# Rows of x turned on VectorE, from quarter rows, in a gated attention and mixture-of-experts kernel

## The reference

```python
router_logits = flat @ router_w.T                 # flat: 4096 rows (xn), 16 experts
topk_w, topk_idx = jax.lax.top_k(softmax(router_logits), 2)
topk_w = topk_w / jnp.sum(topk_w, axis=-1, keepdims=True)
shared = silu(flat @ shared_gate_w) * (flat @ shared_up_w) @ shared_down_w   # inner width 1024
# each expert, on the rows that chose it, inner width 512:
dn = (silu(xs @ gate_w[e]) * (xs @ up_w[e])) @ down_w[e]
routed = zeros.at[sorted_tok].add(sorted_w[:, None] * dn)
output = shared + routed                          # then gated by g_ffn and added to the row
```

## Time and profile before

| | |
|---|---|
| median of 3 runs | 3086.06 us (3083.86 to 3086.15) |
| the profiled execution | 3110.33 us, span 3108.8 us |
| TensorE matmul, busy | 2960.7 us (95%) |
| VectorE, busy | 1638.6 us (53%) |
| ScalarE, busy | 1013.8 us (33%) |
| GpSimd, busy | 595.8 us (19%) |
| mean granted TensorE clock | 0.979 |

### The profile page before, as it was taken

How to read it: one execution, slowest core, us unless ns; L and a number is a source line. 1 busy time by engine, 2 the same in 40 slices (tenths; PEclk the granted TensorE clock), 3 DMA queues, 4 the chain that set the end, 5 groups by cost and what they waited for, 6 DMA issues and landing times.

```text
span 3108.8 us, 48018 instructions
## 1 busy us (share of the span) xinstructions
PE 2960.7 (95%) x17262; PEld 2443.7 (79%) x17263; DVE 1638.6 (53%) x3104; ACT 1013.8 (33%) x1916; POOL 595.8 (19%) x572
## 2 busy tenths in 40 slices
PE   4799999999999988999999999999999999999999
PEld 3687777777878766888888888888888888888887
DVE  3778788887888764333243333332333344444444
ACT  4444444444444412332233333332333331111111
POOL 1333333333343331000000000000000001111111
PEclk6799999999999998999999999999999999999999
DMA  6454445445444534143433333433333324444444
GB/s 192 137 170 137 150 137 176 151 140 158 152 150 142 153 128 152 59 149 128 142 141 136 142 135 142 142 135 142 140 143 135 135 81 158 145 138 159 142 145 145
DMA packets 205721, 441.74 MB, mean 142 GB/s; under 512 B 86784, under 2 KB 87680, under 8 KB 205056
## 3 DMA queue, kind: packets, MB, share of 16 engines
q1 hardware_dynamic: 110544, 333.62, 31.7%
q0 software_dynamic: 24400, 72.96, 7.2%
q10 hardware_dynamic: 70656, 33.56, 4.2%
HBM read 350.72 MB, written 107.18 MB: 147 GB/s over the span
## 4 chain that ended last, share of the span: by engine, by line
PE 59%; DVE 1%; ACT 1%; ACTq 0%; issue 0%; DVEq 0%
PE p_g_b L1532 19%; PE p_up_b L1532 19%; PE p_y_b L1520 17%; PE p_x_b L1500 3%; PE p_h_b L1507 1%; DVE w_lo L1384 1%; ACT w_hi L1327 1%; ACTq L1181 0%; ACTq L1166 0%; DVE x L1440 0%; DVE sg_b L1412 0%; DVE x L1431 0%; ACT th_b L1369 0%; DVE y_b L1442 0%; ACTq L1323 0%
## 5 line engine op out<-in xcount | busy, mean ns | idle before, releaser
L1400 DVE TENSOR_TENSOR ht_lo_b<-p_h_b,ht_hi_b 128x512 fp32r<-128x512 f32 x105 | 72.4, 689 | 544.5 <-ACT ht_hi_b L1339 544.5
L1532 PE MATMUL p_g_b<-w_hi,xt_hi_b 128*128 128x512 f32 x840 | 342.0, 407 | 16.2 <-DVE w_lo L1384 12.9
L1520 PE MATMUL p_y_b<-w_hi,ht_hi_b 128*128 128x512 f32 x840 | 340.1, 405 | 1.9 <-DVE ht_lo_b L1400 1.9
L1412 DVE SCALAR_TENSOR_TENSOR sg_b<-th_b,p_g_b 128x512 f32<-128x512 f32 x105 | 72.1, 687 | 493.5 <-ACT th_b L1369 493.5
L1532 PE MATMUL p_up_b<-w_hi,xt_lo_b 128*128 128x512 f32 x840 | 331.0, 394 | 0.0
L1532 PE MATMUL p_up_b<-w_lo,xt_hi_b 128*128 128x512 f32 x840 | 330.1, 393 | 0.0
L1520 PE MATMUL p_y_b<-w_lo,ht_hi_b 128*128 128x512 f32 x840 | 330.0, 393 | 0.0
L1532 PE MATMUL p_g_b<-w_hi,xt_lo_b 128*128 128x512 f32 x840 | 329.8, 393 | 0.0
L1532 PE MATMUL p_up_b<-w_hi,xt_hi_b 128*128 128x512 f32 x840 | 327.4, 390 | 0.0
L1532 PE MATMUL p_g_b<-w_lo,xt_hi_b 128*128 128x512 f32 x840 | 327.0, 389 | 0.0
L1520 PE MATMUL p_y_b<-w_hi,ht_lo_b 128*128 128x512 f32 x840 | 326.8, 389 | 0.0
(11 more groups left out here) (221 smaller groups left out, 5694.1 us busy)
## 6 DMA issues: line engine op xcount, KB each, us to landing
mid_y<-y_b SPq DMA_DIRECT2D x73, 512.0 KB, 3.2
stage<-mid_g_row SPq DMA_DIRECT2D x64, 512.0 KB, 5.4
stage<-in_eg SPq DMA_DIRECT2D x16, 2048.0 KB
stage<-in_eu SPq DMA_DIRECT2D x16, 2048.0 KB, 15.2
stage<-in_ed SPq DMA_DIRECT2D x16, 2048.0 KB, 19.4
mid_y<-in_x SPq DMA_DIRECT2D x34, 512.0 KB
stage<-in_x SPq DMA_DIRECT2D x32, 512.0 KB
stage<-in_ctx_t ACTq DMA_DIRECT2D x32, 512.0 KB, 8.3
```

Of the source, the lines that this page charges most:

```text
L1400: nc.vector.tensor_tensor(ht_lo[:, :, :], p_h[:, :, :], ht_hi[:, :, :].bitcast(f32), ALU.subtract).then_inc(ht_rdy, 1)
L1412: nc.vector.scalar_tensor_tensor(out=sg[:, :], in0=th[:, :], scalar=1.0, in1=p_g[:, :], op0=ALU.add, op1=ALU.mult).then_inc(silu_step, 1)
L1520: last = nc.tensor.matmul(p_y[n][:, :], a[:, k, :], b[:, GUP + k, w], start=(k == 0 and m == 0), stop=(k == FE // P - 1 and m == 2))
L1532: mm = nc.tensor.matmul(out[:, :], a[:, k, :], w[:, k, o:o + FE], start=(k == 0 and m == 0), stop=(k == KD - 1 and m == 2))
```

## The change

The rows of x are no longer turned on TensorE but on VectorE, in blocks of 32 by 32, each of which stays in its group of 32 partitions. So the parts of a row are spread over the four groups when they are loaded: group a (partitions 32a to 32a + 31) gets quarter a of every row, four tokens to a partition. One instruction then turns all of it, into `x_t` in SBUF, where partition p holds the values 8p to 8p + 7. The weights' rows are loaded in the same order ("(p k) f" in place of "(k p) f"), since value 8p + k now meets slice k.

For this, `idx` is loaded four times, once for each group, and a number 0 to 3 (`quarter`) is added on GpSimd, which gives rows of xn seen as 16384 quarter rows (the lists now hold four times the token). Four gathers of 128 quarter rows of 1 KB follow in place of one of 128 rows of 4 KB. Plain loads of x are four as well, one for each group of 32 partitions. The turn stands in VectorE's body between `h_low` and `silu_up`. `x_high` and `x_low` read `x_t` in place of PSUM. `sg` is gone: silu works in `th`.

```diff
@@ mix_block, end of GpSimd's part
-            pool.dma_start(idx[:, :], t["lists"][0:P, :]).then_inc(idx_in, 16)
-            ge_apart(pool, past, (idx_in, 16), (xn_out, 16 * NCH), (xn_ps, 2 * NCH))
-            nc.gpsimd.indirect_dma_start(
-                out=xn[:, :], out_offset=None, in_=t["xn"],
-                in_offset=bass.IndirectOffsetOnAxis(ap=idx[:, :], axis=0)).then_inc(row0_in, 16)
+            for a in range(4):
+                pool.dma_start(idx[32 * a:32 * a + 32, :], t["lists"][0:P, :].rearrange("(j t) w -> j (t w)", t=4)
+                               ).then_inc(idx_in, 16)
+            ge_apart(pool, past, (quarter_set, 4))
+            pool.wait_ge(idx_in, 64)
+            nc.gpsimd.tensor_tensor(idx_q[:, :], idx[:, :], quarter[:, :], ALU.add).then_inc(idx_rdy, 1)
+            ge_apart(pool, past, (xn_out, 16 * NCH), (xn_ps, 2 * NCH))
+            pool.wait_ge(idx_rdy, 1)
+            for n in range(4):
+                nc.gpsimd.indirect_dma_start(
+                    out=xn[:, 256 * n:256 * n + 256], out_offset=None,
+                    in_=t["xn"].rearrange("c (a d) -> (c a) d", a=4),
+                    in_offset=bass.IndirectOffsetOnAxis(ap=idx_q[:, n:n + 1], axis=0)).then_inc(row0_in, 16)
@@ weights_in
-        eng.dma_start(place, matrix.rearrange("(k p) f -> p k f", p=P)).then_inc(sem, 16)
+        eng.dma_start(place, matrix.rearrange("(p k) f -> p k f" if place.shape[1] == GUP else "(k p) f -> p k f", p=P)
+                      ).then_inc(sem, 16)
@@ ffn_block, plain loads of x (SyncE's load_x, GpSimd's first two)
+            for a in range(4):
+                eng.dma_start(xg_parts[32 * a:32 * a + 32, :, :], xn_quarters[c, a]).then_inc(done, 16)
@@ ffn_block, GpSimd's rows_of
-                    ge_apart(pool, past, (x_in, 16 * i))
-                    pool.dma_start(idx[:, :], list_parts[bass.ds(part, 1)].rearrange("o p w -> (o p) w")
-                                   ).then_inc(idx_in, 16)
-
-                ge_apart(pool, past, (idx_in, 16 * i + 16 if c is None else 0), (xt_ps, i))
+                    for a in range(4):
+                        pool.dma_start(idx[32 * a:32 * a + 32, :],
+                                       list_parts[bass.ds(part, 1)].rearrange("o (j t) w -> (o j) (t w)", t=4)
+                                       ).then_inc(idx_in, 16)
+                    ge_apart(pool, past, (idx_in, 64 * i + 64))
+                    ge_apart(pool, past, (x_in, 64 * i))
+                    nc.gpsimd.tensor_tensor(idx_q[:, :], idx[:, :], quarter[:, :], ALU.add).then_inc(idx_rdy, 1)
+                    ge_apart(pool, past, (idx_rdy, i + 1))
+                ge_apart(pool, past, (x_turned, i))
@@ ffn_block, VectorE
+            def turn_x(i, c):
+
+                ge(dve, xt_rdy, 2 * i)
+                if c is None or isinstance(c, int) and c == 0:
+                    dve.wait_ge(x_in, 64 * i + 64)
+                else:
+                    dve.wait_ge(xs_in, 64 * c)
+                nc.vector.transpose(x_t[:, :, :].rearrange("p k (j t) -> p t k j", t=4),
+                                    xg_parts[:, :, :].rearrange("p t (i k) -> p t k i", k=KD)).then_inc(x_turned, 1)
...
                 if prev:
                     h_low(i)
+                if not last:
+                    turn_x(i + 1, c)
                 silu_up(i)
@@ ffn_block, TensorE
                 mm.then_inc(gu_ps, 1)
-                if not last:
-                    turn_x(i + 1, c)
                 if prev:
                     down(i, e - 1 if first else e)
```

More of the change, by code:

```diff
@@ L166, in mix_block @@
         cnt_ps, cnt_step = sem("cnt_ps"), sem("cnt_step")
-        idx, idx_in, row0_in = keep["idx"], keep["idx0_in"], keep["row0_in"]
+        idx, idx_q, quarter = keep["idx"], keep["idx_q"], keep["quarter"]
+        idx_in, idx_rdy, row0_in = keep["idx0_in"], keep["idx0_rdy"], keep["row0_in"]
         gu0_hi, gu0_split = keep["gu0_hi"], keep["gu0_split"]
         xn_out = sem("xn_out")
-        fill_in = sem("fill_in")
+        fill_in, quarter_set = sem("fill_in"), sem("quarter_set")
         wp_in = [sem(f"wp_in{n}") for n in range(SLOTS)]
@@ L660, in stage_w @@
                                             ).then_inc(w_split, 1)
+                if part == 1 and b == 0 and j == 2:
+                    for a in range(4):
+                        nc.vector.memset(quarter[32 * a:32 * a + 32, :], a).then_inc(quarter_set, 1)
             def stage_l(part, b, j):
@@ L1131, in ffn_block @@
         base_row = sb("base_row", [P, D])
-        p_x = [ctx.enter_context(nc.psum_tensor(f"p_x{n}_{tag}", [P, 4, P], f32)) for n in range(2)]
         p_g = ctx.enter_context(nc.psum_tensor(f"p_g_{tag}", [P, FE], f32))
@@ L1137, in ffn_block @@
         r0, r1 = keep["x1"][:, 0, :], keep["x1"][:, 1, :]
-        idx, starts_i = keep["idx"], keep["starts_i"]
+        idx, idx_q, quarter, starts_i = keep["idx"], keep["idx_q"], keep["quarter"], keep["starts_i"]
         first_row = sb("first_row", [P, NE])
@@ L1341, in x_high @@
             def x_high(i):
-                act.wait_ge(xt_ps, i + 1)
+                act.wait_ge(x_turned, i + 1)
                 for n in range(2):
-                    nc.scalar.activation(xt_hi[:, 4 * n:4 * n + 4, :], p_x[n][:, :, :], ACT.Copy).then_inc(xt_hi_rdy, 1)
+                    nc.scalar.activation(xt_hi[:, 4 * n:4 * n + 4, :], x_t[:, 4 * n:4 * n + 4, :],
+                                         ACT.Copy).then_inc(xt_hi_rdy, 1)
             def y_left(q):
@@ L1483, in finish @@
                 join(q, c)
+            turn_x(0, None)
             x_low(0)
@@ L1490, in _ @@
             trio = ((xt_hi, w_hi), (xt_lo, w_hi), (xt_hi, w_lo))
-            def turn_x(i, c):
-                if c is None or isinstance(c, int) and c == 0:
-                    pe.wait_ge(x_in, 16 * i + 16)
-                else:
-                    pe.wait_ge(xs_in, 16 * c)
-                for k in range(KD):
-                    last = nc.tensor.transpose(p_x[k // 4][:, k % 4, :], xg[:, k * P:(k + 1) * P], ident[:, :])
-                last.then_inc(xt_ps, 1)
             def turn_h(i):
@@ L1559, in build @@
         for n, s, dt in (("stage", [P, PIECES, D], f32), ("w_hi", [P, PIECES, D], f32r), ("w_lo", [P, PIECES, D], f32r),
-                         ("xn", [P, D], f32), ("x1", [P, 2, D], f32), ("idx", [P, 1], i32), ("starts_i", [P, 2, NE + 1], i32)):
+                         ("xn", [P, D], f32), ("x1", [P, 2, D], f32), ("idx", [P, 4], i32), ("quarter", [P, 4], i32), ("idx_q", [P, 4], i32), ("starts_i", [P, 2, NE + 1], i32)):
             keep[n] = ctx.enter_context(nc.sbuf_tensor(n, s, dt))
-        for n in ("idx0_in", "row0_in", "gu0_hi", "gu0_split"):
+        for n in ("idx0_in", "idx0_rdy", "row0_in", "gu0_hi", "gu0_split"):
             keep[n] = ctx.enter_context(nc.semaphore(n))
```

35 lines of the change are left out of this document (20 added, 15 removed).

## The result

The changed kernel took 2988.85 us in the median of four runs (2987.68 to 2991.48), the kernel before 3084.96 us on the same chip: ratio 0.9693, 95% interval 0.9682 to 0.9705. That is 96.1 us off, where 84.3 were forecast.

A forecast was written before the change was run, and what follows sets the result against it. TensorE's own work was taken to bound the kernel; -89.6 us for removed transposes and +4.6 at the start gave -85.0, scaled to 84.3 off 3086.06: 3001.7 us, 8-in-10 range 2991 to 3027.

The forecast's parts named there:

- the removal per tile: TensorE, routed stage: without eight transposes the down products move up 0.87 us in 103 tiles, 89.6 us in all.
- the overlap at the two ends: TensorE, either end of a tile's transposes: by how overlap is counted, the removal could be 0.79 to 0.95 us.
- The turn: VectorE, between ht_lo and silu: one turn of x a tile, taken as 2.0 us, bounds 1.2 to 5.5, costing nothing.
- The cover: VectorE's idle time before silu plus room behind it: a turn up to 7.0 us, 6.1 in a first tile, is free.
- Rival D: VectorE: strides make the turn slow, each us past 7.0 paid 103 times, about 3210 us at 9; chance 0.03.
- The gathers: GpSimd: four gathers a tile, 1.27 us apart, land 9.0, at worst 12.2 us after a turn, within 14.9; cost nothing.
- Rival C: GpSimd: each gather lasts its full landing time, so the period becomes 20.4 us and the time near 3245; chance 0.04.
- their ring: Routed tiles: a turn frees the next gathers, whose landing allows the next turn; decides from a period of 18.1 us on.
- Rival B: Tiles beside weight loads: x is late only there, 30 us if two tiles of 15 experts lose 1 us; chance 0.08.
- The start: Routed stage's opening: idx loads, gathers and turn are not hidden, first gate product +4.6 us, bounds +3 to +8.
- nothing given: Routed stage's second tile: transposes lie beside the tanh and silu chain in a pause that stays, so removing them gains nothing.
- The scaling to the median by 0.9922: Whole kernel: unprofiled median is 0.9922 of the profiled time, so -85.0 us became 84.3 off 3086.06.

The follow-up runs named there:

- the longer index buffers: Kernel before with idx as wide as in the changed kernel and quarter and idx_q allocated but unused: ratio 0.9958 to the kernel before.
- three turns: Changed kernel with every tile's turn of x done three times over on VectorE, 6.9 us in place of 2.27: 3064.06 us.
- the run with eight gathers: Changed kernel with four spare gathers, into a buffer that nothing reads, ahead of the four in each routed tile: 3017.76 us.
- the one with twelve: Changed kernel with eight spare gathers, into a buffer that nothing reads, ahead of the four in each routed tile: 3322.0 us.
- the other chip: Changed kernel itself, repeated on the chip of later experiments: ratio 0.969 to the kernel before.
- the changed kernel with the shorter start: Changed kernel with idx's four groups filled by one transfer and tile 1's list fetched ahead of the routed stage: 3001.58 us beside the changed kernel's 3003.78.
- the kernel before with 128 bytes: Kernel before with longer index buffers and 64 bytes more of unused memory, its operands moved by 128 bytes in all: ratio 1.0097 to the kernel before.
- 512 bytes added: Changed kernel with 512 bytes of unused memory ahead of x_t: ratio 0.9672 to the kernel before.
- 96 bytes: Changed kernel with 96 bytes of unused memory ahead of quarter: ratio 0.9861 to the kernel before.
- its repeat: Kernel before, unchanged, profiled again: ratio 0.9994.

## Why the prediction was right, and where its range failed

The way of the change and its mechanism were right, and the experiments bear them out; the step that failed is the size of the first term, the removal per tile.

**The removal.** The step "the down products move up by the whole 0.87 us" held, in 103 tiles. The term was mis-sized: tiles gave 0.99, not 0.87 (0.95 at most), so -101.6 us and not -89.6. Of the 0.12 missing, 0.08 is the place in memory, of which the forecast said nothing, and 0.00 to 0.04 the overlap at the two ends, for which its bound of 0.95 had room. That is, it took the longer index buffers for bytes without a price. The eight transposes cost 0.87 to 0.91 us by experiment, 0.11 each. The Trainium skill, "TensorE: Matmul & The Clock Gate", Part 4, gives about 275 ns for one of bf16 in a kernel; the record's length agrees (272 ns), the price of one in a row of eight does not, and 2.2 us a tile were not there to gain.

**The turn.** 2.27 us where 2.0 were taken, inside the bounds, wholly in the idle stretch. The cover was 7.4 us (forecast 7.0) in a plain tile, and less at an expert's change, where three turns already cost. Rival D would have needed 7.5 us or more. Taking the strides' 1.02 us away left the tile at 16.81 us, so the turn's length does not set the time. The Trainium skill, "Advanced Engine Details and Errata", SBUF Cachelines, has the penalty without a figure. The strided row that I held against it shows little of one: 345 ns less the fixed 154 is 1.5 ns an element for 1.2. The turn does show one: strides of 32 and 16 bytes took 1.0 ns an element on top of 1.2; which of the two strides costs it, no run tells.

**The gathers.** Issue at 1.27 us apart, x late in no plain tile, as forecast. Rival C fell: twice as many cost nothing in a plain tile, and only with twelve does their ring set the period throughout. Rival B's direction was right for eight and twelve gathers, not for four.

**The start.** Forecast +4.6, measured +4.0 to the first product. That it came so near is partly luck. The forecast let x's landing, 4.4 us behind the last gather's start, set the first turn; what set it was the end of the block, 7.2 us behind that start (0.95 of issue and 6.24). And it put the last gather 11.7 us behind the first idx load, where it was 8.6. The two errors nearly cancel. What failed is the silence on the tile after: the forecast costed the first tile's x and then counted tile 1 as "nothing given", where its chain (four idx loads, four gathers, of which one took 1.89 us beside w_lo, a landing of 6.48 us beside weight loads) is longer than tile 0's products. It cost 3.7 us more, 0.9 of it through the clock. On the other chip tile 1's period was 17.94 us, 1.9 more than 16.07, so the size varies. The last tile gave 1.7 back: the last 24 down products took 7.41 us before, in a stretch granted 0.77 of the clock, and 5.78 after, granted 1.00. The change did not do that: both values turn up in both kernels (7.33 us at 0.77 in the changed kernel with the shorter start, 5.87 us at 1.00 in the kernel before with 128 bytes), in all four behind a pause of 1.8 to 1.9 us.

**The ledger** in the profiled executions: stretch of 104 periods 1768.8 - 1866.7 = -97.9 (which is -101.6 and tile 1's +3.7), the first stage's last store to the first tanh +3.96 - 0.32 = +3.6, behind the last tanh 17.5 - 19.2 = -1.7. The sum is -96.0, and the medians differ by 96.1; so close a match is partly chance, since the -1.7 is the clock's and not the change's. From the forecast's -85.0 to it, the removal makes -12.0, tile 1 +3.7, the start -1.0 and the clock in the last tile -1.7. The scaling to the median by 0.9922 was needless: as far as the profiles tell, what the profiled execution of before had over its median lay in the first stage, since the routed stage took 1866.7 us in it and again when it was repeated. It moved the forecast by 0.7 us. The low end, 2991, rested on 0.95 us a tile with +3 at the start; 0.99 was outside it.

## What to carry to other kernels

Work taken from the engine that bounds comes back at its price in the chain, and what takes its place is free up to a room that can be read beforehand; but read the room in the tightest tile, not the plain one, walk the first tiles of a stage one by one, and count what is issued ahead of a block's end, since the engines wait for that. When buffers change size, ask what moves behind them: here 32 bytes decide over 1.5% of the time, half of what this whole change gave, so two kernels are compared at equal places, or a spread of places is tried with unused memory.

## What the runs showed of the hardware

A product of 512 columns starts every 227.6 to 228.9 or every 233.1 to 234.2 ns by the place of the routed buffers in memory. Ten kernels fit a rule by the remainder of the address by 512 bytes, and one by 256 as well. I know no reason for it.

An indirect gather's issue on GpSimd takes 0.95 us, and up to 1.97 us while VectorE subtracts two operands in SBUF to make w_lo. In the run with eight gathers 44 of 109 issues with their middle in w_lo stayed under 1.9 us, and in the one with twelve 49 of 108, so not every one is hit. The Trainium skill, "Advanced Engine Details and Errata", GPSIMD Details, says that GpSimd shares a read and a write interface with VectorE and conflicts with its instructions of two SBUF inputs; the trace agrees in part: the long issues all lie in w_lo, which has two such inputs, and lost 1.02 us, less than one of the split's eight pieces (1.2 us). But xt_lo is the same operation on two inputs in SBUF, half as long, and none of the 62, 65 and 68 issues beside it in the changed kernel and in the runs with eight and twelve gathers took 1.5 us.

A TensorE that had paused for 5.53 us restarted at half the clock (1.2 GHz), with products 0.43 us apart in place of 0.23 for the first 5.3 us, 15 in 6 us. The length of the pause alone does not decide it: behind 5.03 us there were 14 products in 6 us (512 bytes added) and behind 4.73 us there were 20 (96 bytes). Behind the same 1.9 us there were 19 in the kernel before and in its repeat, and 29 with its longer index buffers, at a granted clock of 1.00.

In the fourteen runs with the changed start, the second block began 6.24 or 6.25 us behind the end of GpSimd's last issue in the first.
